# Two ternary weight steps moved from the first head pair of the differential attention to the end of the cross attention

## The reference, cut to what matters

```
x = x + L0_xattn(layernorm(x), ctx, itok, ...)        # cross attention in windows
x = x + L0_attn(layernorm(x), Wq, Wk, Wv, Wo, lambda) # differential attention, 16 heads of 128
x = x + L0_ffn(layernorm(x), w_gate_up, w_proj)       # ternary weights

def ternary_quant(w_fp32, g=64):
    w = w_fp32.astype(bfloat16)
    w_g = w.reshape(-1, g)
    scale = clip(mean(abs(w_g), axis=-1, keepdims=True), 1e-08, None)
    q = clip(round(w_g / scale), -1, 1)
    w_hat = (q * scale).reshape(w.shape)
    return w + stop_gradient(w_hat - w)
```

## Time and profile before

| | us |
|---|---|
| median of three runs | 891.83 (891.07 to 893.16) |
| the profiled execution | 891.05 |
| its span | 889.1 |
| TensorE busy | 808.3 (91% of the span) |
| VectorE busy | 614.2 (69%) |
| ScalarE busy | 489.9 (55%) |
| GpSimd busy | 170.2 (19%) |
| mean granted TensorE clock | 0.966 of full |

### The profile page before, as it was taken

One profiled execution on the slowest core, in us unless ns is written; L12 is line 12 of the kernel. 1 busy time (PEld: TensorE's weight loads), 2 busy tenths in 40 slices (PEclk: granted clock), 3 DMA queues, 4 the chain that ended last, 5 costly groups with the idle time before them and its releaser, 6 DMA issues.

```text
span 889.1 us, 14007 instructions
## 1 busy us (share of the span) xinstructions
PE 808.3 (91%) x5335; PEld 617.1 (69%) x5335; DVE 614.2 (69%) x1068; ACT 489.9 (55%) x817; POOL 170.2 (19%) x168
## 2 busy tenths in 40 slices
PE   3999999999799869999999998999978659999996
PEld 3897555777688758787878887445754537888885
DVE  6764786667765579999999987347798696343333
ACT  3565874323655687877787743445656535333331
POOL 2236550000255300000000000223131230212112
PEclk9999999999799999999999999999998878999999
DMA  8724566770123634434453005041034600212101
GB/s 308 257 108 150 185 207 247 274 248 16 46 93 98 217 119 143 140 99 127 133 166 102 19 25 194 0 168 69 1 106 162 243 20 24 72 48 72 48 1 48
DMA packets 49867, 106.80 MB, mean 120 GB/s; under 512 B 6714, under 2 KB 26098, under 8 KB 46220
## 3 DMA queue, kind: packets, MB, share of 16 engines
q1 hardware_dynamic: 48908, 95.33, 32.0%
q0 software_dynamic: 896, 10.62, 3.0%
HBM read 100.69 MB, written 5.25 MB: 119 GB/s over the span
## 4 chain that ended last, share of the span: by engine, by line
PE 78%; DVE 10%; ACT 7%; issue 2%; DMA 1%; SPq 0%; POOL 0%; ACTq 0%; DVEq 0%
PE banks L41 16%; PE banks L43 15%; PE banks L42 15%; PE banks L2181 6%; PE banks L364 2%; PE banks L1327 2%; PE banks L1748 2%; PE banks L2211 2%; PE banks L2212 2%; PE banks L1357 1%; PE banks L1188 1%; PE banks L1964 1%; PE banks L2012 1%; PE banks L1330 1%; PE banks L243 1%
## 5 line engine op out<-in xcount | busy, mean ns | idle before, releaser
L157 POOL TENSOR_TENSOR w_low<-w_raw,w_high 128x256 fp32r<-128x256 f32 (+2 forms) x44 | 58.0, 1326 | 147.2 <-ACT w_high L153 144.3
L153 ACT CAST w_high<-w_raw 128x1024 fp32r<-128x1024 f32 (+2 forms) x74 | 56.8, 779 | 29.0 <-PE banks L43 21.6
L41 PE MATMUL banks<-da_xT_high,w_high 128*128 128x512 f32 (+1 forms) x136 | 53.1, 390 | 0.0
L41 PE MATMUL banks<-hf_xhh,w_high 128*128 128x512 f32 (+1 forms) x136 | 52.0, 383 | 0.1
L42 PE MATMUL banks<-hf_xhl,w_high 128*128 128x512 f32 (+1 forms) x136 | 52.0, 382 | 0.0
L43 PE MATMUL banks<-hf_xhh,w_low 128*128 128x512 f32 (+1 forms) x136 | 52.0, 382 | 0.0
L43 PE MATMUL banks<-da_xT_high,w_low 128*128 128x512 f32 (+1 forms) x136 | 51.8, 381 | 0.0
L42 PE MATMUL banks<-da_xT_low,w_high 128*128 128x512 f32 (+1 forms) x136 | 51.5, 379 | 0.0
L2851 POOL TENSOR_TENSOR hf_hl<-hf_h,hf_hh 128x512 fp32r<-128x512 f32 x16 | 24.3, 1520 | 123.8 <-ACT hf_hh L2907 123.8
L2061 POOL MEMSET ff_acc<- 128x512 f32 x1 | 0.5, 529 | 239.4 <-DVE x_res L1656 239.4
L2915 DVE TENSOR_TENSOR hf_downW_l<-dw_w,hf_downW_h 128x512 fp32r<-128x512 f32 x16 | 11.2, 697 | 50.7 <-ACT hf_downW_h L2867 50.7
(11 more groups left out here) (439 smaller groups left out, 2486.7 us busy)
## 6 DMA issues: line engine op xcount, KB each, us to landing
cs_rows<-in_ctx SPq DMA_DIRECT2D x24, 1024.0 KB, 5.0
tw_raw<-in_L_ffn_w_gate_up SPq DMA_DIRECT2D x16, 512.0 KB, 4.2
hf_raw<-in_L_ffn_W_up SPq DMA_DIRECT2D x16, 512.0 KB, 3.5
w_raw<-in_L_xattn_W_o SPq DMA_DIRECT2D x8, 512.0 KB
w_raw<-in_L_attn_Wq SPq DMA_DIRECT2D x8, 512.0 KB
w_raw<-in_L_attn_Wk SPq DMA_DIRECT2D x8, 512.0 KB
w_raw<-in_L_attn_Wv SPq DMA_DIRECT2D x8, 512.0 KB
w_raw<-in_L_attn_Wo SPq DMA_DIRECT2D x8, 512.0 KB
```

Of the source, the lines that this page charges most:

```text
L41: nc.tensor.matmul(out, a[0], b[0], start=start, stop=False)
L153: self.nc.scalar.copy(self.wh[k][:, 0:cols], self.raw[k][:, 0:cols]).then_inc(self.split_hi[k], 1)
L157: self.nc.gpsimd.tensor_tensor(self.wl[k][:, 0:cols], self.raw[k][:, 0:cols], self.wh[k][:, 0:cols].bitcast(F32), ALU.subtract).then_inc(s ...
```

## The change

Of steps 0 and 1, the loads, casts and magnitudes go among the last output products of the cross attention: SP issues the two loads in front of the first Wq load, behind a wait for the window attention's last scores (`o_out`); ScalarE does cast and magnitude of both in front of its split of Wq, and the two wide copies behind its split of Wv; TensorE makes the four mean products in front of the 24 matmuls of the last output product, into banks 0 to 3; GpSimd fills the mean matrix behind its last split of the cross attention. TensorE waits for the two wide copies before it transposes for the norm. Loads 2 and 3 go in front of SP's wait for the cross attention's end. Behind the norm, ScalarE takes sign 0 in front of lambda, and VectorE quantises step 0 in front of lambda; step 1 is quantised in front of the first softmax and no longer behind it. Sign 1, and casts and magnitudes 2 to 4, are spread otherwise over the first pair. A wait of TensorE in the second pair for the second wide copy goes.

```diff
--- before.py
+++ after.py
@@ -1160,7 +1160,7 @@
             dve.wait_ge(self.y_add, m + 1)
             following.vector_stats(ch, m)
 
-    def tensor(self, pe):
+    def tensor(self, pe, ternary):
         c, nc = self.c, self.c.nc
         f, K8 = self.f, self.KEYS
         self.ln.tensor(pe)
@@ -1374,6 +1374,9 @@
             slot, fill = self.slot_y(k, i)
             pe.wait_ge(c.split_lo[slot], fill)
             pe.wait_ge(self.v_lo, 4 * i + 2 * k + 2)
+            if n == PAIRS - 1:
+                for s in range(2):
+                    ternary.tensor(pe, s, 2 * s)
             for m in range(M):
                 for h in range(2):
                     ins = mm3(nc, c.bank[:, 4 + m, :], tuple(part[h][:, m * P:(m + 1) * P] for part in self.vo[k]),
@@ -1430,19 +1433,19 @@
             c.fill(sp, k, self.f[k] + 1 + i, [(c.raw[k].rearrange("p (h n) -> p h n", h=2), src)])
 
     def sync_first(self, sp):
+        for s in range(2):
+            self.tw.load(sp, s)
         for k in range(4):
             self.load(sp, 0, k)
+        for s in (2, 3):
+            self.tw.load(sp, s)
 
     def sync(self, sp):
         d, tw = self.c.dram, self.tw
         sp.dma_start(self.mask[:, :, :], d["causal"].unsqueeze(1).broadcast_to([P, M, S])).then_inc(self.in_, 16)
         sp.dma_start(self.lam[:, 0, :], d["L0_attn_lambda_init"].unsqueeze(0).broadcast_to([P, H])).then_inc(self.in_, 16)
-        for s in range(2):
-            tw.load(sp, s)
         for k in range(3):
             self.load(sp, 1, k)
-        for s in (2, 3):
-            tw.load(sp, s)
         for i in range(PAIRS):
             if i < PAIRS - 1:
                 tw.load(sp, 3 * i + 4)
@@ -1465,14 +1468,18 @@
         nc = self.c.nc
         for h in range(2):
             nc.gpsimd.memset(self.a[h][:, :, :], 0.0).then_inc(self.zero, 1)
-        self.tw.gpsimd(pool)
         pool.wait_ge(self.c.ln_xn, M * (self.ln.u + 1))
         for k in (1, 3):
             self.c.split_low(pool, k, self.f[k] + 1)
 
     def scalar_first(self, act):
+        for s in range(2):
+            self.tw.scalar_cast(act, s)
+            self.tw.scalar_abs(act, s)
         for k in self.FIRST:
             self.c.split_high(act, k, self.f[k] + 1)
+        for s in range(2):
+            self.tw.scalar_wide(act, s, 2 * s)
         self.ln.scalar_ready(act)
 
     def scalar(self, act):
@@ -1480,6 +1487,7 @@
         self.ln.scalar_std(act)
         c.split_high(act, 1, self.f[1] + 1)
         self.ln.scalar_turned(act)
+        tw.scalar_sign(act, 0)
         act.wait_ge(self.in_, 32)
         nc.scalar.activation(self.lam[:, 1, :], self.lam[:, 0, :], ACT.Exp, scale=-1.0).then_inc(self.lam_e, 1)
         c.split_high(act, 3, self.f[3] + 1)
@@ -1520,25 +1528,17 @@
             if i:
                 out_high(i - 1)
             if i == 0:
-                tw.scalar_cast(act, 0)
-                tw.scalar_abs(act, 0)
+                tw.scalar_sign(act, 1)
                 queries(0, 0)
-                tw.scalar_cast(act, 1)
-                tw.scalar_abs(act, 1)
+                tw.scalar_cast(act, 2)
+                tw.scalar_abs(act, 2)
                 queries(0, 1)
                 c.split_high(act, 0, self.f[0] + 2)
-                tw.scalar_wide(act, 0, 4)
-                tw.scalar_sign(act, 0)
+                tw.scalar_cast(act, 3)
                 keys(0, 0)
-                tw.scalar_cast(act, 2)
-                tw.scalar_abs(act, 2)
+                tw.scalar_abs(act, 3)
                 keys(0, 1)
-                tw.scalar_wide(act, 1, 6)
-                tw.scalar_sign(act, 1)
-                tw.scalar_cast(act, 3)
-                tw.scalar_abs(act, 3)
                 tw.scalar_cast(act, 4)
-                tw.scalar_abs(act, 4)
             else:
                 tw.scalar_cast(act, 3 * i + 2)
                 tw.scalar_abs(act, 3 * i + 2)
@@ -1559,6 +1559,8 @@
                 c.split_high(act, 1, self.f[1] + 2 + i)
             values(i, 0)
             values(i, 1)
+            if i == 0:
+                tw.scalar_abs(act, 4)
             exponentials(i, 0)
             values(i, 2)
             exponentials(i, 1)
@@ -1583,6 +1585,7 @@
     def vector(self, dve, ch, following):
         c, nc, tw = self.c, self.c.nc, self.tw
         v = nc.vector
+        tw.vector_quantise(dve, ch, 0)
         dve.wait_ge(self.lam_e, 1)
         ch(v.tensor_scalar(self.lam[:, 2, :], self.lam[:, 1, :], 1.0, None, ALU.add))
         ch.wait()
@@ -1635,17 +1638,15 @@
             last = i == PAIRS - 1
             if i:
                 out_low(i - 1)
-            tw.vector_quantise(dve, ch, 3 * i)
+            if i:
+                tw.vector_quantise(dve, ch, 3 * i)
             if not last:
                 low(0, self.f[0] + 2 + i)
-            if i:
-                tw.vector_quantise(dve, ch, 3 * i + 1)
+            tw.vector_quantise(dve, ch, 3 * i + 1)
             softmax(i)
             if not last:
                 low(1, self.f[1] + 2 + i)
                 low(2, self.f[2] + 2 + i)
-            if i == 0:
-                tw.vector_quantise(dve, ch, 1)
             tw.vector_quantise(dve, ch, 3 * i + 2)
             if i:
                 low(3, self.f[3] + 1 + i)
@@ -1701,8 +1702,6 @@
                         cols = slice(h * HD, (h + 1) * HD)
                         ins = mm3(nc, c.bank[:, h, :], (wh[:, j, cols], wl[:, j, cols]), (self.to.xTh[:, j, :], self.to.xTl[:, j, :]), j == 0, j == C - 1)
                     ins.then_inc(self.proj, 1)
-                if i == 0:
-                    tw.tensor(pe, k, 4 + 2 * k)
             if i:
                 pe.wait_ge(self.o_lo, 2 * i)
             for h in range(2):
@@ -1728,8 +1727,6 @@
             pe.wait_ge(self.v_out, 4 * i + 4)
             tw.tensor(pe, 3 * i + 2, 0)
             if i:
-                if i == 1:
-                    pe.wait_ge(tw.wide_ok, 2)
                 project(i - 1)
             if i < PAIRS - 1:
                 pe.wait_ge(tw.wide_ok, 3 * i + 3)
@@ -3105,6 +3102,7 @@
                 sp.dma_start(core.x[:, :, :], dram["x"].rearrange("m p d -> p m d")).then_inc(core.x_in, 16)
                 sp.dma_start(core.onehot[:, :], dram["onehot"]).then_inc(core.x_in, 16)
                 window.sync(sp)
+                sp.wait_ge(window.o_out, window.G // 4)
                 diff.sync_first(sp)
                 after_window(sp)
                 diff.sync(sp)
@@ -3138,6 +3136,8 @@
             def _(pool):
                 ch = Chain(pool, core.pool_step)
                 window.gpsimd(pool, ch)
+                pool.wait_ge(window.ol_, 2 * PAIRS)
+                ternary.gpsimd(pool)
                 diff.gpsimd_first(pool)
                 after_window(pool)
                 diff.gpsimd(pool)
@@ -3196,7 +3196,8 @@
             def _(pe):
                 pe.wait_ge(core.const_in, 16 * 3)
                 pe.wait_ge(core.identb_ok, 1)
-                window.tensor(pe)
+                window.tensor(pe, ternary)
+                pe.wait_ge(ternary.wide_ok, 2)
                 after_window(pe)
                 diff.ln.tensor(pe)
                 diff.tensor(pe)
```

## The result

| | before | changed |
|---|---|---|
| median of 22 runs each | 892.38 (889.17 to 893.95) | 886.98 (884.83 to 897.36) |
| span of the profiled execution | 889.1 | 884.5 |
| TensorE / VectorE / ScalarE busy | 808.3 / 614.2 / 489.9 | 808.0 / 616.7 / 489.6 |

The ratio is 0.9949, with a 95% interval of 0.9935 to 0.9964, so 3.2 to 5.8 us are gained at 892.38 us. The medians alone are 5.4 us apart. The same work is done; what went is idle time of TensorE, and time that it spent at a lower granted clock.

The account below looks back on a forecast made before the run. TensorE holds most of the chain; ScalarE's queue stalls it 3.40 us in the first pair. Terms -5.95 (including +0.93) and -0.55 sum to -6.5 us, giving 885.3 us; own range 883.6 to 887.0, 8-in-10 range 883.0 to 888.8.

Parts of the forecast that it names:

- Parts 1 and 2: Early ternary loads, and ScalarE's two early casts and magnitudes before the norm: no cost, 0.8 us slack.
- Part 3: Four mean products before the cross attention's last output product delay the path by 0.93 us.
- Part 4: Behind the norm: with step 1 quantised first, the first softmax still begins at 317.0; POOL's split may cost 2.4 us.
- Part 5: First pair: value products lose the 3.40 us pause and run at full clock; fourth value copy starts 5.95 us earlier.
- The sixteen products: Sixteen 128-column products of the first pair, starting at 328.0: a partly higher clock gains 0.55 us.
- The case in which they stay slow: First pair's sixteen products run at the lower clock level again, gaining 0 there; the gain would be 5.95 us.
- The bound of 1.75: Upper limit for the first pair's sixteen products at full clock: 3.68 - 1.93, up to 1.75 us gained.
- rival B: Following pairs: VectorE's chain sets the period, so the early start is lost; within 1.8 us of before, chance 0.09.
- A: First pair: VectorE becomes the bound, softmax 2 to 4.5 us late; gain only 2 to 4.5 us, 888.6, chance 0.16.
- C: Slower: last output product waits for the second magnitude; a load landing at 296.5 gives 892.8 us; chance 0.05.
- D: More gain: full clock in the sixteen products, fewer slow stretches in the norm; 884.2 to 882.5 us, chance 0.04.
- Behind the attention nothing is tied to absolute time: After the differential attention, the rest of the program keeps its duration, so the 6.5 us gain carries to the end.

Follow-up runs that it names:

- The loads alone: Kernel before, with only the first two ternary loads put in front of the first Wq load: 890.66 us, ratio 0.9989.
- the spreading alone: Kernel before, with magnitude 3 and cast and magnitude 4 moved behind value copies of the first pair: 889.44 us, ratio 0.9970.
- the kernel with both waits filled: Changed kernel, mean products behind cross attention's last output product, seven unread products before differential attention's last output product, ten in the norm's wait: 879.91 us, ratio 0.9859.
- the wait filled: Changed kernel, with seven unread 512-column products in the 1.84 us wait before the differential attention's last output product: 886.00 us, ratio 0.9919.

## Why the prediction was right

The forecast was 885.3, which is 6.5 us under a kernel before of 891.83. Measured are 886.98 against 892.38: 5.4 us between the medians, 3.2 to 5.8 by the ratio, and ratios of 0.9940 and 0.9941 on other chips (4.1 to 6.7 and 3.7 to 7.0 us). The sign and the mechanism are as told, and the pairs gain what was forecast; the program as a whole gains about one us less. That 886.98 lies inside a range that ends at 887.0, by 0.02 us, is luck. Point by point:

- **What bounds.** Right: ScalarE's queue in the first pair held TensorE. The loads alone moved nothing; the spreading alone took nearly all of the pause away (0.22 us left of 3.40), with no work removed.
- **Parts 1 and 2** at nothing: right. The loads-only kernel shows it, and no wait stands in front of the mean products. Wv was 1.5 us late where I allowed 3.
- **Part 3, +0.93:** mis-sized. It measured 0.64 (three traces) and 0.88 (one).
- **Part 4:** the softmax at 317.0 was 317.24, by a smaller margin than I had thought. I let POOL's split hold step 0 by up to 2.4 us; it was 2.1 (2.79 less 0.69). The timeline of POOL (GpSimd) has the split in the same time:

```profile
307.19 2.83 POOL L157 TENSOR_TENSOR w_low<-w_raw,w_high 128x1024 fp32r<-128x1024 f32 x1 [3.74 <-ACT w_high L153]
```

VectorE's operation started at 307.79 and ended at 310.58, 0.56 behind the end of POOL's. Four of its five forerunners ran with POOL idle, the fifth had started (307.06) before POOL's; none was stretched, while POOL's took 2.83 us against 2.41 for the same split in the trace of before. The Trainium skill has this rule ("SBUF — State Buffer", SBUF: two separate sides): VectorE, in an operation with two inputs in SBUF as here, and GpSimd share a port pair that is locked for a whole instruction, and the one that starts later stands still. The trace agrees with it, 2.79 against 0.69 us.
- **Part 5, -5.95 at the fourth value copy:** 321.86 against 327.55 is -5.69, and -6.1 counted from B as a mean. The forecast had both halves of it, the pause and the full clock in the value products behind (4.63 against 2.89 us). The last wait of TensorE in the pair ends at 326.93 (forecast 326.8), the sixteen products begin at 328.69 (328.0).
- **The sixteen products, -0.55:** right in size, but the duration of one row was a poor measure. They took 2.50 to 3.19 us in the four traces of the change, and without the change 3.68, 3.18 and 2.05: where the slow clock falls varies on both sides. From sixteen 0 to sixteen 1, which holds whatever the clock costs there, it is 30.1 to 30.4 us before and 29.2 to 29.9 in the change, 0.7 us less in the mean. The case in which they stay slow, which gives 5.95 in all and which the prediction set beside the rule of the Trainium skill ("TensorE: Matmul & The Clock Gate", What's actually happening), was half a microsecond too small: the mean over traces is 6.45. The bound of 1.75 took 3.68 from the timeline and 1.93 from the chain; with the timeline's 2.05 it is 1.63.
- **Sum, -6.5:** 6.45 at sixteen 7. It passed all eight pairs, and rival B is refuted (sixteen 0 gains 5.84, sixteen 7 gains 6.45). A is too: the softmax started in time. C never came up; its figures don't fit together either, since a landing at 296.5 would be 9.2 us behind 287.3 and so give 885.3 + 9.2 = 894.5, not 892.8. D is not seen in the change; the full clock in the norm, which it named, is what the kernel with both waits filled brought about, at 879.91.
- **"Behind the attention nothing is tied to absolute time": the step that failed.** From sixteen 7 to the root the gain shrinks from 6.45 to 5.65. In two of four traces the wait of 1.84 us in front of the last output product is followed by a lower granted clock (0.77) and 1.6 us more; half of 1.6 is the 0.8. The three traces without the change had the same wait and no fall. So the 0.8 us is what these traces show, and not a settled cost of the change: 2 of 4 against 0 of 3 may be chance. With the wait filled the product ran at 1.00 (one trace in one kernel, again in one with more edits). The rest of the program takes 341.2 against 340.9, which leaves 5.4 us, the distance of the medians; that they agree so well is luck too, since single traces of one kernel differ by more than 1 us there.

## What to carry to other kernels

Look for the instruction that frees the bank or buffer for which the matrix engine waits, and at what stands in front of it in its own engine's queue: moving work behind it (3.5 us here, with nothing taken away) can be worth as much as moving work out of the stage (3.7 at the end of the pair), and since both shorten the same wait, the two together give less than their sum (5.8). What is moved early must also be finished early, or the buffers that it holds stop its successor a pair later (2.1 us). A part that loses elsewhere must be read where its own effect lies, not at the program's end. And a wait of a few microseconds on the matrix engine may cost more than its length, by the clock behind it (1.7 us more behind the 3.40 here, 1.6 us in some executions behind the 1.84): measure it with dummy products in the wait.

## What the hardware showed that I had not expected

- Identical code behind an identical wait of 1.84 us ran at a granted clock of 0.77 in some executions and at 1.00 in others (7.35 and 5.74 us for 24 products).
- Ten products that nobody reads (2.64 us in a wait of 3.6) took the lower clock away from the norm behind them (0.51 to 1.00), and with it came a stage 400 us later that ran at 1.00 instead of 0.69; both together are 5.1 us between two traces, 0.6% of the program. The Trainium skill ("TensorE: Matmul & The Clock Gate", What's actually happening) says that activity lifts the throttle, which agrees with the first (0.51 to 1.00); no run here shows why the second followed.
- Idle time need not show as idle: a VectorE operation beside GpSimd's is listed as busy for 2.79 us instead of 0.69, so that the busy total of VectorE rose by 2.5 us (614.2 to 616.7) with no work added; 2.1 of them are this operation.
